# Attention and feed-forward on one core: new orders at the entry and the end of the attention's double steps

## The reference

```python
x = x + attn(layernorm(x));  x = x + ffn(layernorm(x))
def attn(x):
    q, k, v = split(conv1d(x, conv_w, width 3) + conv_b)            # 256 each, blocks of 128 tokens
    qh, kh, vh = q @ wq + bq, k @ wk + bk, v @ wv + bv              # 16 heads of 64
    p = softmax(where(causal, qh * 64**-0.5 @ kh.T, -1e9))          # in each block of 128
    return ((p @ vh) @ wo + bo) @ proj_w + proj_b
def ffn(x):                                                          # dense 1024x1024 + 4 LoRA experts
    y = x @ W_base.T + b_base;  z = x @ A[active].T
    alpha = softmax(log(prior + eps) + x @ router_W.T + router_b)
    return y + sum_e alpha_e * 2 * (z_e @ B_e.T)
```

## Time and profile before

| | us |
|---|---|
| median of 3 runs (lowest, highest) | 812.07 (810.99, 812.50) |
| the profiled execution | 811.95 |
| its span, first to last instruction | 810.2 |
| TensorE busy | 779.5 (96%) |
| VectorE (DVE), ScalarE (ACT), GpSimd (POOL) busy | 491.9, 384.4, 196.4 |

### The profile page before, as it was taken

The page is one execution under the profiler, slowest core; times in us unless marked ns, Lnnn a source line. Parts: engine busy times, 40 slices in busy tenths (PEclk is TensorE's granted clock), DMA queues, the critical chain, the costliest instruction groups (busy, mean ns, idle before and its releaser), DMA issues.

```text
span 810.2 us, 14378 instructions
## 1 busy us (share of the span) xinstructions
PE 779.5 (96%) x5266; PEld 704.1 (87%) x5266; DVE 491.9 (61%) x1392; ACT 384.4 (47%) x1052; POOL 196.4 (24%) x184
## 2 busy tenths in 40 slices
PE   4999999999999889999999999999899999999996
PEld 3898888777878778999999999898789999999996
DVE  6999994889877566454545454646775444444441
ACT  5953343244335777676767676767741111111010
POOL 2300102222330234343434343443201010000000
PEclk9999999999999999999999999999999999999999
DMA  8746735433346140403071424020423131323201
GB/s 333 264 131 195 253 101 190 171 116 119 118 149 235 40 157 1 145 1 144 2 299 54 99 106 144 1 106 2 163 72 104 53 104 54 105 59 98 78 27 52
DMA packets 41370, 94.04 MB, mean 116 GB/s; under 512 B 9299, under 2 KB 18387, under 8 KB 40020
## 3 DMA queue, kind: packets, MB, share of 16 engines
q1 hardware_dynamic: 38996, 84.73, 31.2%
q0 software_dynamic: 2304, 8.39, 2.5%
HBM read 66.63 MB, written 26.08 MB: 114 GB/s over the span
## 4 chain that ended last, share of the span: by engine, by line
PE 68%; DVE 21%; ACT 6%; issue 3%; POOL 2%; DMA 0%; DVEq 0%; ACTq 0%; POOLq 0%
PE net_psum L63 16%; PE net_psum L65 16%; PE net_psum L64 16%; PE net_psum L1299 4%; PE net_psum L1310 3%; PE net_psum L1322 3%; DVE x_lo L899 2%; ACT pr L640 2%; PE net_psum L1350 2%; PE net_psum L1351 2%; PE net_psum L1352 2%; PE net_psum L1385 2%; POOL raw L486 1%; DVE raw L906 1%; DVE ua L861 1%
## 5 line engine op out<-in xcount | busy, mean ns | idle before, releaser
L63 PE MATMUL net_psum<-fw_hi,xT_hi 128*128 128x354 f32 (+1 forms) x384 | 126.1, 328 | 0.4 <-DVE fw_lo L1105 0.4
L65 PE MATMUL net_psum<-fw_hi,xT_lo 128*128 128x354 f32 (+1 forms) x384 | 124.4, 324 | 0.0
L64 PE MATMUL net_psum<-fw_lo,xT_hi 128*128 128x354 f32 (+1 forms) x384 | 124.2, 324 | 0.0
L510 POOL TENSOR_TENSOR pr<-pr,rrec 128x512 f32<-128x512 f32 x64 | 66.5, 1040 | 210.0 <-DVE rrec L978 207.0
L640 ACT ACTIVATE pr<-pr,negmax 128x128 f32<-128x128 f32 x256 | 99.0, 395 | 1.4 <-DVE negmax L970 1.4
L1239 PE MATMUL net_psum<-ua,wa 128*128 128x256 f32 x384 | 83.8, 379 | 0.5 <-DVE ua L864 0.5
L1239 PEld LDWEIGHTS net_psum<-ua,wa 128*128 128x128 f32 x384 | 72.6, 190 | 10.4 <-issue 0.7
L970 DVE CUSTOM_DVE_ANT_0 pr<-net_psum,mask 128x128 f32<-128x128 f32 x256 | 57.1, 286 | 40.1 <-PE net_psum L1299 40.1
L63 PE MATMUL net_psum<-c_hi,wqk_hi 128*128 128x256 f32 x256 | 74.5, 291 | 4.8 <-ACT kf L649 3.3
L63 PE MATMUL net_psum<-x_hi,w_hi 128*128 128x512 f32 x192 | 76.8, 400 | 1.7 <-DVE w_lo L913 1.5
L486 POOL TENSOR_TENSOR raw<-raw 128x512 f32<-128x512 f32 x24 | 36.8, 1533 | 161.3 <-ACT raw L589 161.3
(11 more groups left out here) (177 smaller groups left out, 1790.6 us busy)
## 6 DMA issues: line engine op xcount, KB each, us to landing
wa<-in_conv_w SPq DMA_DIRECT2D x24, 512.0 KB, 4.0
raw<-in_conv_w SPq DMA_DIRECT2D x24, 384.0 KB, 3.8
xn<-in_x SPq DMA_DIRECT2D x16, 512.0 KB, 10.1
xr<-in_x SPq DMA_DIRECT2D x8, 1024.0 KB, 5.0
x_scratch<-xr SPq DMA_DIRECT2D x8, 1024.0 KB, 4.1
x1t<-x_scratch SPq DMA_DIRECT2D x16, 512.0 KB, 4.1
out<-y POOLq DMA_DIRECT2D x16, 512.0 KB, 5.0
c_raw<-c_scratch SPq DMA_DIRECT2D x7, 768.0 KB, 4.7
```

The costliest lines, as they stand in the source:

```text
L63: pe.matmul(out, w_hi, x_hi, start=first, stop=False)
L64: pe.matmul(out, w_hi, x_lo, start=False, stop=False)
L65: return pe.matmul(out, w_lo, x_hi, start=False, stop=last)
L510: pool.tensor_tensor(pr[:, jj % 4], pr[:, jj % 4], rrec[:, jj % 4].unsqueeze(2).to_broadcast([P, UN, P]), ALU.mult).then_inc(s["p_ready"], 1)
```

## The change

It moves calls within the engines' lists, and one operation from one engine to another; what is computed stays the same.

- Queries and keys have three banks: 7 and 9 go to bank 6. A block waits only for the copy of the block that used its bank before.
- TensorE: at D = 1 block 2 runs ahead of the scores. ACT: at D = 2 block 4 is copied ahead of the turned p; at D = 2 to 4 the odd block is copied between the two sets of exponentials; the halves of wo's high part run at D = 1 and 2, both `c_high` of group 1 at D = 2.
- `c_low` of group 1 goes from POOL to DVE (`first_c_low`, D = 3). `last_sums` 1 and 2 run at D = 1, 3 at D = 2.
- POOL: both `bias_sum` of a group run at q = 3, ahead of the multiplications.
- Dense weights: chunks 0 and 1 are split at D = 28 and 29 instead of 30 and 31, 2 and 3 (ACT: to 4) before D = 32, and so on. At D = 32 ACT runs exponentials 62 ahead of the turned p, and DVE runs the second `unit_out` between the reciprocals.
- The end on TensorE: p x v 60 and 61, turns 62 and 63, tile 0's turns, output sums 60 and 61.

Banks of the queries and keys:

```diff
+        qk_bank = {b: psum[:, b].rearrange("p (k t) -> p k t", k=2) for b in (0, 3, 6)}
+        QK_HOME = {1: 3, 3: 3, 7: 6, 9: 6}
         def qk_acc(J):
-            return qk_side if J in (1, 3) else qkp
+            return qk_bank[QK_HOME.get(J, 0)]
+        def qk_before(J):
+            return max((j for j in range(J) if QK_HOME.get(j, 0) == QK_HOME.get(J, 0)), default=-1)
```

POOL:

```diff
             def attention_pair(D):
                 g, q = D // DG, D % DG
+                if 0 <= g - 1 < NG - 1 and q == 3:
+                    bias_sum(g - 1, 0)
+                    bias_sum(g - 1, 1)
                 for jj in pair_of(D - SC):
...
-                if g == 0 and q == 3:
-                    c_low(1, 0)
-                    c_low(1, 1)
                 if 0 < g and g + 1 < NG and q in (2, 3):
                     c_low(g + 1, q - 2)
-                if 0 <= g - 1 < NG - 1 and q in (2, 3):
-                    bias_sum(g - 1, q - 2)
```

ACT:

```diff
+                if D == 2:
+                    queries_keys(2 * D)
+                if D == ND:
+                    exponentials(2 * (D - SC))
                 for jj in pair_of(D - TR):
                     turned_out(jj)
                 for h in range(2):
-                    if D < ND and h == 0:
+                    if D < ND and D != 2 and h == 0:
                         queries_keys(2 * D)
-                    if pair_of(D - SC):
+                    if D in (2, 3, 4) and h == 1:
+                        queries_keys(2 * D + 1)
+                    if pair_of(D - SC) and (D, h) != (ND, 0):
                         exponentials(2 * (D - SC) + h)
                     if 0 < g and g + 1 < NG and q == 1:
                         c_high(g + 1, h)
-                    if D < ND and h == 1:
+                    if D < ND and D not in (2, 3, 4) and h == 1:
                         queries_keys(2 * D + 1)
-                if D in (2, 3):
-                    c_high(1, D - 2)
                 if D == 2:
+                    c_high(1, 0)
+                    c_high(1, 1)
+                if D in (1, 2):
+                    k = D - 1
                     act.wait_ge(s["wo_loaded"], 16)
-                    for k in range(2):
-                        act.activation(wo_hi[:, 4 * k:4 * k + 4], wo_raw[:, 4 * k:4 * k + 4], ACT.Copy).then_inc(s["wo_hi_ready"], 1)
+                    act.activation(wo_hi[:, 4 * k:4 * k + 4], wo_raw[:, 4 * k:4 * k + 4], ACT.Copy).then_inc(s["wo_hi_ready"], 1)
...
-                if D in (ND - 2, ND - 1):
-                    high_dense(D - (ND - 2))
+                if D in (ND - 4, ND - 3):
+                    high_dense(D - (ND - 4))
             high_dense(2)
             high_dense(3)
+            high_dense(4)
             attention_pair(ND)
...
+            high_dense(5)
+            attention_pair(ND + 1)
             tile_xT(0)
-            high_dense(4)
-            attention_pair(ND + 1)
-            high_dense(5)
+            high_dense(6)
             attention_pair(ND + 2)
-            high_dense(6)
             high_dense(7)
```

DVE:

```diff
+            def first_c_low(h):
+                m = slice(3 * h, 3 * h + 3)
+                dve.wait_ge(s["c_hi_ready"], h + 1)
+                dve.tensor_tensor(c_lo[:, 1, m], c_raw[:, m], c_hi[1][:, m], ALU.subtract).then_inc(s["c_lo_ready"], 1)
...
+                if D == 3:
+                    first_c_low(0)
+                    first_c_low(1)
+                if D in (ND - 3, ND - 2):
+                    low_dense(D - (ND - 3))
+                unit_out(D, 0)
                 if D == ND:
-                    low_dense(2)
-                unit_out(D, 0)
-                for jj in pair_of(D - SC):
-                    reciprocals(jj)
-                unit_out(D, 1)
+                    reciprocals(2 * (D - SC))
+                    unit_out(D, 1)
+                    reciprocals(2 * (D - SC) + 1)
+                else:
+                    for jj in pair_of(D - SC):
+                        reciprocals(jj)
+                    unit_out(D, 1)
+                if D == 1:
+                    last_sums(1)
+                    last_sums(2)
                 if D == 2:
-                    last_sums(1)
-                if D == 3:
-                    last_sums(2)
                     last_sums(3).then_inc(s["cy_ready"], 1)
...
-                if D in (ND - 2, ND - 1):
-                    low_dense(D - (ND - 2))
+            low_dense(2)
+            low_dense(3)
             attention_pair(ND)
-            low_dense(3)
+            low_dense(4)
+            attention_pair(ND + 1)
             dve.wait_ge(s["az_split_hi"], 1)
...
             low_xT(0)
-            low_dense(4)
-            attention_pair(ND + 1)
             low_dense(5)
             attention_pair(ND + 2)
```

TensorE (`run_unit` with k = 0 first):

```diff
+                    elif D == 5:
+                        pe.wait_ge(s["qk_ready"], 10)
...
-                wait(pe, s["qk_ready"], J if J > 4 else J - 1)
+                wait(pe, s["qk_ready"], qk_before(J) + 1)
+                if J == 7:
+                    emptied(pe, J // 2, 0)
...
+                if D in (1, 2):
+                    queries_keys(2 * D)
                 if D == 2:
-                    queries_keys(2 * D)
                     run_unit(D, 0)
...
-                if D < ND and D != 2:
+                if D < ND and D not in (1, 2):
                     queries_keys(2 * D)
...
             for D in range(ND + 1):
                 attention_pair(D)
+            for jj in pair_of(ND - 2):
+                head_outputs(jj)
+            for jj in pair_of(ND - 1):
+                turns(jj)
             tile_transposes(0)
-            attention_pair(ND + 1)
+            for jj in pair_of(ND - 2):
+                output_sums(jj)
             for jj in pair_of(ND - 1):
                 head_outputs(jj)
             dense(0, 0)
```

More of the change, by code:

```diff
@@ L247, in network @@
         M1, M2, M3, M4 = 0, 1, 2, 3
-        qkp = psum[:, 0].rearrange("p (k t) -> p k t", k=2)
         scp = psum[:, 1:3]
         ptp = (psum[:, 3], psum[:, 7])
-        qk_side = psum[:, 3].rearrange("p (k t) -> p k t", k=2)
+        qk_bank = {b: psum[:, b].rearrange("p (k t) -> p k t", k=2) for b in (0, 3, 6)}
+        QK_HOME = {1: 3, 3: 3, 7: 6, 9: 6}
         op = psum[:, 4].rearrange("p (j b t) -> p j b t", j=2, b=GB)
```

## The result

The changed kernel takes 803.21 us (median of 4 runs, 803.08 to 803.35), beside 811.53 us (810.51 to 812.50) of the kernel before on the same chip: a ratio of 0.9896 with a 95% interval of 0.9884 to 0.9908, or 8.3 us. The profiled execution took 803.25 us with a span of 801.5 us. Its profile (0.996) is of the second kind, so it shows a little more to gain (8.7 us) than the medians do.

The account below looks back on a forecast made before the run. TensorE was taken to run dense except for waits at the attention's entry and end; 811.95 less 4.8 (entry) and 3.8 (end) gave 803.35, so 803.5 us for the median, range 800.2 to 806.8.

Parts of the forecast that it names:

- Entry: First to eleventh queries-and-keys block: new queue orders cut TensorE's waits, 39.4 us for 44.2, so 4.8 us gained.
- turn 5: Entry, D = 4: wo_lo(1) on DVE goes before POOL's p 5, so TensorE's turn waits 1.6 us in place of 0.5.
- Middle: Steps between entry and end: scores stay 10.1 us apart with no wait of TensorE, so no time gained or lost.
- cost nothing: Middle: POOL's bias sums moved ahead of p's multiplications at q = 3, seven times, priced at 0 with 2.3 us cover.
- End: D = 31 to the last output sums: earlier chunk splits, full clock and shorter waits, 3.8 us gained.
- D = 31: End: without chunk 0's split on DVE, masks and a_lo come 1.9 us earlier and the wait goes, 1.1 us gained.
- New wait at D = 32: End: TensorE's second unit waits 1.7 us for the turned p behind exponentials 62 on ACT, clock staying at 1.00.
- full clock: End: granted clock 1.00 instead of 0.50 gains 1.4 us, 1.1 in the output sums and 0.3 behind them.
- shorter waits: End: TensorE's waits up to the last output sums shrink, 1.3 us of the 3.8 gained.
- Fuller gain: Rival: POOL wins the turn at D = 4, ACT early enough at D = 32; 5.9 + 5.5, 800.7 us; chance 0.17.
- half gain: Rival: lower clock behind the D = 32 wait, or DVE's queue at D = 2 to 4 slips; 806.8 us; chance 0.20.
- Slower: Rival: bias_sum waits for the load of xr, delaying POOL's multiplications and turns seven times; 817 us; chance 0.03.

Follow-up runs that it names:

- entry only: The changed kernel with its end (steps 29 to 34) as in the kernel before, bias sums still moved: 806.72 us, ratio to before 0.9937.

## Why the prediction was right, and where it wasn't

803.5 was forecast, 803.21 came. The sum was made for before's profile and its median of 812.07; with one more execution that median is 811.53, so of the forecast 8.6 us 8.3 came. Its steps, one by one:

**Entry, 4.8 forecast, 5.1 measured.** The eleventh block was put at 291.6 and started at 291.51, from a first block 0.25 later. The waits that were kept, each with the end of the row before it: turn 3, 0.6 forecast and 0.6 measured (TensorE was free at about 272.6); output sums of D = 3, 1.2 and 1.3; turn 5, 1.6 and 1.1; turn 7, 0.7 and 0.8. VectorE and GpSimd took turns as in the earlier trace rows, whole instruction by whole instruction with VectorE first: wo_lo(1) ran to 282.0 and product 5 ended at 282.9, where 281.95 and 283.0 stood in the text. The term off is turn 5's: TensorE came half a microsecond later than assumed, so the same product made it wait less.

**Middle, 0 forecast, 0 measured** in time spent there, 261.82 against 261.87. But the reason was incomplete. The step "cost nothing" looked at who waits behind the bias sums in their *new* place, and not at whom they held up in the *old* one: VectorE's splits of D = 30 and 31. It was in the prediction's own rows, the 3.04 us of the earlier trace rows "beside a bias sum". That the number of the end came out right all the same is luck in this respect: the sum there has the splits of chunks 2 and 3 done 2.5 us after the start of D = 32 (568.4 to 570.9). That is their time without a bias sum beside them, 2.49 in the changed kernel; with one beside them it was 4.31, in both runs that had it. The whole was priced rightly and one of its parts at 0 that is worth 3.9 in it; a reader who had kept all but this edit would have lost half the gain.

**End, 3.8 forecast, 3.8 measured.** D = 31, 1.1 forecast and 1.2 measured: 11.35 became 10.14. New wait at D = 32: 1.7 forecast, 1.51 and the end of the row before it measured, released by ACT's pT, at a clock of 1.00 as assumed. Last chunk: 0.6 and 0.38. No wait at turn 63, where 0.3 was allowed. By the full clock, 1.4 forecast and 1.5 measured (output sums 2.86 and 1.59 us, p x v 1.12 and 1.02, dense (0, 0) 4.94 and 4.79). By shorter waits, 1.3 forecast and 1.0 measured from the start of D = 32 to the output sums (12.94 and 11.91). The reason given for this term was incomplete: the text named tile 0's turns as cover, and they carry 0.65 of the end; what else took before's 2.29 away is by the rows the place of the heads' outputs on ScalarE and VectorE. The new wait belongs to one of the end's orders alone, exponentials 62 first: the prediction had the end 1.7 better without the wait (5.5 for 3.8), and undoing that order gave 1.1.

**The rivals.** "Fuller gain" needed GpSimd to win the turn at D = 4 and no wait at D = 32; neither came. The half gain, with the lower clock behind the wait of D = 32, is what the changed kernel comes to as soon as the bias sums go back (807.08 beside the rival's 806.8). "Slower" did not happen: no product waited for xr, the sums ended at 557.8 and the next product started at 560.65.

## What to carry to other kernels

Price a moved instruction at both places: what it delays where it arrives, and what it releases where it leaves, on the other engine of the shared port above all. Undo each part of a change alone in the *final* kernel: the end's new orders took 0.5 us from their stage without the bias sums' move and 3.8 with it, and one part (exponentials first) turned out to cost 1.1. An operation that holds up another engine goes where that engine has nothing to do, not merely later.

## What the runs showed of the hardware

A GpSimd operation of 2.37 us stretched two VectorE splits from 2.36 to 4.18 us, though it began only 0.4 us ahead of them. Two GpSimd products with a VectorE split between them took 3.02 us, two without it 2.04; one that began 0.16 us behind a split took 1.93, one alone 1.04. The Trainium skill, "SBUF — State Buffer", section "SBUF: two separate sides", has the lock for whole instructions, and these rows agree. Who goes next when both wait the rows add: VectorE, at 280.9 as in the earlier trace rows. In both places it had also been waiting for longer, so they don't tell a preference for VectorE from the order of asking.

The granted clock stayed at 1.00 behind the waits of 1.12 and 1.51 us and was 0.50 behind those of 2.10 (entry only, 579 to 581 us), 2.29, 2.88 and 3.33, in the executions that were profiled. Between the executions of one and the same kernel it moved the time by 2.1 us (805.50 to 807.65). So a wait that grew by 1.8 us cost 2.3 to 4.4 us, 3.9 in the median.
